# Graph network of 64 graphs: conv2 as nine quarter-rate products over eight graphs at a time

## What is computed

```python
h  = relu(bn2(conv1d(relu(bn1(conv1x1(hT))), conv2_w, pad=8)) + hT)     # x_conv, 17 taps over nodes
s  = h @ w_se.T + b_se;  A = exp(-|s_n - s_m|^2) * adj                   # 3 features
nmp = A @ relu(h @ w_msg.T + b_msg)
r, z, n = GRU gates of [x_conv, nmp] (w_ih) and h (w_hh)
x1 = x + (1 - z) * n + z * h
out = x1 + adj @ (relu(layernorm(x1)) @ weight) + bias
```

## Time and profile before

| | us |
|---|---|
| median of 3 runs | 410.81 (408.74 to 412.92) |
| the profiled execution, its span | 412.3 |
| TensorE busy, by the page | 372.0 (90%) |
| VectorE busy | 327.8 (80%) |
| GpSimd busy | 182.9 (44%) |
| ScalarE busy | 134.7 (33%) |

### The profile page before, as it was taken

One profiled execution on the slowest core, in us unless ns is written; L12 is line 12 of the kernel. 1 busy time (PEld: TensorE's weight loads), 2 busy tenths in 40 slices (PEclk: granted clock), 3 DMA queues, 4 the chain that ended last, 5 costly groups with the idle time before them and its releaser, 6 DMA issues.

```text
span 412.3 us, 7317 instructions
## 1 busy us (share of the span) xinstructions
PE 372.0 (90%) x2460; PEld 335.4 (81%) x2460; DVE 327.8 (80%) x920; ACT 134.7 (33%) x232; POOL 182.9 (44%) x191
## 2 busy tenths in 40 slices
PE   8489497999999999999999999999999999999974
PEld 7377296897979798897979798888979797997953
DVE  5975579679897979879797979879787979778564
ACT  3222132424324242424333342424333242424031
POOL 3973218045271807254361817164461817072402
PEclk9999689999999999999999999999999999999995
DMA  8700000020202020010202020010200000000000
GB/s 305 240 0 0 0 2 0 2 79 2 78 1 76 0 76 0 17 59 0 76 0 76 0 76 0 29 47 0 76 0 25 0 25 0 25 2 14 13 25 26
DMA packets 7933, 15.19 MB, mean 37 GB/s; under 512 B 1008, under 2 KB 1392, under 8 KB 7920
## 3 DMA queue, kind: packets, MB, share of 16 engines
q1 hardware_dynamic: 7632, 14.42, 10.2%
q10 hardware_dynamic: 288, 0.61, 0.4%
HBM read 10.83 MB, written 4.19 MB: 36 GB/s over the span
## 4 chain that ended last, share of the span: by engine, by line
PE 58%; DVE 31%; issue 5%; ACT 3%; DVEq 1%; DMA 1%; POOL 0%; POOLq 0%; ACTq 0%
PE pAC L296 5%; PE pAC L297 5%; PE pAC L298 5%; PE pF L392 4%; PE pH L436 3%; PE pR L296 3%; PE pH L447 3%; DVE h_hi L699 3%; DVE st L625 3%; DVE h_lo L701 3%; DVE st L648 3%; PE pR L298 3%; PE pR L297 3%; PE pZ L297 3%; PE pZ L296 3%
## 5 line engine op out<-in xcount | busy, mean ns | idle before, releaser
L296 PE MATMUL pAC<-c_hi,conv_hi 128*128 128x264 f32 (+1 forms) x288 | 86.8, 301 | 2.5 <-DVE c_lo L713 2.5
L297 PE MATMUL pAC<-c_lo,conv_hi 128*128 128x264 f32 (+1 forms) x288 | 84.0, 292 | 0.0
L298 PE MATMUL pAC<-c_hi,conv_lo 128*128 128x264 f32 (+1 forms) x288 | 83.7, 291 | 0.0
L860 POOL TENSOR_TENSOR base_e<-hTb,A 128x256 f32<-128x256 f32 x16 | 12.7, 794 | 155.7 <-ACT A L531 155.7
L296 PEld LDWEIGHTS pAC<-c_hi,conv_hi 128*128 128x128 f32 x288 | 56.0, 194 | 2.9 <-issue 2.9
L298 PEld LDWEIGHTS pAC<-c_hi,conv_lo 128*128 128x128 f32 x288 | 55.9, 194 | 0.0
L297 PEld LDWEIGHTS pAC<-c_lo,conv_hi 128*128 128x128 f32 x288 | 55.9, 194 | 0.0
L296 PE MATMUL pB<-c_hi,conv_hi 128*128 128x256 f32 x128 | 37.9, 296 | 1.4 <-DVE conv_lo L617 1.4
L297 PE MATMUL pB<-c_lo,conv_hi 128*128 128x256 f32 x128 | 36.7, 287 | 0.0
L298 PE MATMUL pB<-c_hi,conv_lo 128*128 128x256 f32 x128 | 36.6, 286 | 0.0
L572 ACT ACTIVATE msg<-msg_t 128x512 f32<-128x512 f32 x16 | 10.1, 632 | 76.6 <-DVE msg_t L748 76.6
(11 more groups left out here) (187 smaller groups left out, 1015.8 us busy)
## 6 DMA issues: line engine op xcount, KB each, us to landing
x_all<-x_in SPq DMA_DIRECT2D x16, 256.0 KB, 2.8
adj_all<-adj_in SPq DMA_DIRECT2D x16, 256.0 KB, 3.0
...
```

The costliest lines, as they stand in the source:

```text
L296: pe.matmul(acc, w_hi, m_hi, start=start, stop=False)
L297: pe.matmul(acc, w_hi, m_lo, start=False, stop=False)
L298: return pe.matmul(acc, w_lo, m_hi, start=False, stop=stop)
L860: pool.tensor_tensor(base_e[:], phase[:, :, :, 0], A2[:, :, 0:HALF], ALU.add)
```

## The change

conv2 is split twice into even and odd: four phases of nodes, so nine quarter-rate products (X22, X12, X21, X23, X32, X11, X13, X31, X33) with 4 or 5 taps each, 40 taps, each over 8 graphs x 32 columns, three passes: 120 matmuls for eight graphs. They come as pairs in the two banks pP and pQ. Their inputs are differences of phases: px (8 arrays of 128 x 8 x 36) made by `pre` in five instructions on GpSimd (for the first eight graphs on VectorE), rounded by ScalarE in five instructions (`split_hi`) and the low parts made by VectorE in five (`split_lo`). The weights of the products are sums of taps, 37 arrays of 128 columns in place of 25, made on GpSimd, rounded on ScalarE, split on VectorE. The outputs are joined by `s22`, `s12`, `s32` on ScalarE, one instruction on VectorE and four on GpSimd (`base`), then `conv_out` on VectorE, `conv_round` on ScalarE, `conv_lo_out` on VectorE, each in two halves.

The loop has steps of eight graphs (groups a, b in front, p, q in the middle, pp, qq at the back), `for t in range(-1, NS + 1)` with NS = 8: t = -1 has a front alone, t = 0 no back, t = 7 no front, t = 8 a back alone. Nodes are laid phase-major by the host in x, adj and out, so every operand of a product lies in runs of 32. x lies in a ring of eight groups and adj in a ring of six, each slot with its own semaphore. The high part of h is written by ScalarE from PSUM and the low part by VectorE from PSUM. The message bias comes by two matmuls of 264 columns for each group, so the two additions on VectorE go. `left` and `right` have 128 partitions, with zeros below. The second norm's scaling is four instructions on ScalarE in place of four on VectorE and one on ScalarE. The gate weights are split on VectorE. The special order of t = 0 and the halves of the last steps go. `masked`, `pairs`, `right_rows`, `residual`, `finish`, `blend_start`, `blend_end`, `normalise1`, `apply1`, `normalise2` are the old operations on one group each; `with_bias` adds the last bias, `scale1` and `scale2` are the powers.

The products of conv2, before and after:

```diff
-            def conv2_taps(par, product, lo, hi):
-
-                taps = TO if product == 1 else TE
-                acc = (pAC[:, 0:GG * HA], pB[:, 0:W // 2], pAC[:, 0:W // 2])[product]
-                start, width = ((0, HA), (1, HALF), (1, HALF))[product]
-                for k in range(lo, hi):
-
-                    w = k if product == 0 or k == TO and product == 2 else (TE + k if product == 1 else TAPS + k)
-                    last = split_product(acc, conv_hi[:, w * D:(w + 1) * D], conv_lo[:, w * D:(w + 1) * D],
-                                         c1_hi[par][:, product, :, start + k:start + k + width],
-                                         c1_lo[par][:, product, :, start + k:start + k + width],
-                                         start=k == 0, stop=k == taps - 1)
...
+            def product(acc, side, x, weights):
+                for j, w in enumerate(weights):
+                    last = split_product(acc[:, side * CG * QN:(side + 1) * CG * QN],
+                                         conv_hi[:, w * D:(w + 1) * D], conv_lo[:, w * D:(w + 1) * D],
+                                         cx_hi[:, x, :, j:j + QN], cx_lo[:, x, :, j:j + QN],
+                                         start=j == 0, stop=j == len(weights) - 1)
                 return last
...
+            def four(first, more=False):
+                return list(range(first, first + 4)) + ([T16] if more else [])
```

TensorE, the step of eight graphs (the lines taken out are those of the step shown above):

```diff
+            def step(t):
+                a, b, p, q, pp, qq = 2 * t + 2, 2 * t + 3, 2 * t, 2 * t + 1, 2 * t - 2, 2 * t - 1
+                front, middle, back = t + 1 < NS, 0 <= t < NS, t >= 1
+                if t == -1:
                     pe.wait_ge(ident_set, 1)
                     keep_clock(17)
+                if front:
                     x_turn(a)
+                if t == -1:
                     keep_clock(9)
...
+                if back:
+                    o_turn(pp)
+                if middle:
+                    if t == 0:
+                        pe.wait_ge(w_split, 2)
+                    have(pe, cxlo_set, 5 * t + 1)
+                    have(pe, ct_set, 2 * t)
+                    product(pP, 0, X22, four(M22, True))
+                if front:
+                    conv1(a)
+                    messages(a)
+                    x_turn(b)
+                if middle:
+                    have(pe, cxlo_set, 5 * t + 2)
+                    product(pP, 1, X12, four(M12, True)).then_inc(f_done[0], 1)
+                if back:
+                    o_turn(qq)
+                if front:
+                    conv1(b)
+                    messages(b)
                     rows_turn(a)
...
+                if middle:
+                    if t == 0:
+                        pe.wait_ge(w_split, 3)
+                    have(pe, ct_set, 2 * t - 1)
+                    product(pQ, 0, X21, four(M21, True))
+                if front:
                     distances(a)
+                if back:
+                    adj_h2(pp)
+                if middle:
+                    have(pe, cxlo_set, 5 * t + 3)
+                    product(pQ, 1, X23, four(M23)).then_inc(f_done[1], 1)
+                if front:
+                    rows_turn(b)
+                if back:
+                    layer2(pp)
+                if middle:
+                    have(pe, s1_set, t + 1)
+                    product(pP, 0, X32, four(M32)).then_inc(f_done[2], 1)
+                if back:
+                    adj_h2(qq)
+                if front:
+                    distances(b)
                     neighbour_sums(a)
...
+                if middle:
+                    if t == 0:
+                        pe.wait_ge(w_split, 5)
+                    have(pe, cxlo_set, 5 * t + 5)
+                    have(pe, t_set, t + 1)
+                    product(pQ, 0, X11, four(A0) + [T16])
+                if back:
+                    layer2(qq)
+                if middle:
+                    product(pQ, 1, X13, four(A2)).then_inc(f_done[3], 1)
+                if front:
+                    neighbour_sums(b)
+                if middle:
+                    have(pe, s32_set, t + 1)
+                    product(pP, 0, X31, four(A1))
+                    product(pP, 1, X33, four(A3)).then_inc(f_done[4], 1)
+                    for g in (p, q):
+                        gates_h(g)
+                        gates_n(g)
+                        gates_c(g)
```

ScalarE, the part of its step behind the messages of group b:

```diff
+                if back:
+                    second(qq)
+                if front:
+                    decay(a)
+                if t == -1:
+                    round_w(3)
+                    round_w(4)
+                if back:
+                    turned_up(pp)
+                if front:
+                    left_rows(b)
+                if front and t >= 0:
+                    split_hi(t + 1, 0)
+                    split_hi(t + 1, 1)
+                if middle:
+                    have(act, f_done[2], t + 1)
+                    have(act, sumO_set, t)
+                    act.activation(s32[:], pP[:, 0:CG * QN], ACT.Identity, bias=bn_half[:, 0:1],
+                                   scale=bn_a[:, 1:2]).then_inc(s32_set, 1)
+                if back:
+                    turned_up(qq)
+                if front:
+                    decay(b)
+                    sums_hi(a)
+                if front and t >= 0:
+                    split_hi(t + 1, 2)
+                if t == -1:
+                    split_hi(0, 3)
+                    split_hi(0, 4)
+                    act.wait_ge(gate_loaded, 16)
+                    act.activation(gate_hi[:], gate, ACT.Copy).then_inc(gate_rounded, 1)
+                if front:
+                    sums_hi(b)
+                if middle:
+                    conv_round(t, 0)
+                    hidden_gate(p)
+                    conv_round(t, 1)
+                if front and t >= 0:
+                    split_hi(t + 1, 3)
+                    split_hi(t + 1, 4)
+                if middle:
+                    reset_gate(p)
+                    candidate(p)
+                    update_gate(p)
+                    hidden_gate(q)
+                    reset_gate(q)
+                    update_gate(q)
```

The differences of phases (k = 1 to 5), and VectorE:

```diff
+        def pre(eng, t, k):
+            if k == 1:
+                have(eng, c1_set, 2 * t + 2)
+            elif k > 3:
+                have(eng, pre_set, 5 * t + 3)
+            have(eng, cxlo_set, 5 * t)
+            if k == 1:
+                last = eng.tensor_tensor(px[:, X12:X21 + 1], c1[:, 1:3], c1[:, 3:4].to_broadcast([128, 2, CG, QP]),
+                                         ALU.subtract)
+            elif k == 2:
+                last = eng.tensor_tensor(px[:, X32:X23 + 1, :, 0:QP - 1], c1[:, 0:3:2, :, 1:QP],
+                                         c1[:, 3:4, :, 0:QP - 1].to_broadcast([128, 2, CG, QP - 1]), ALU.subtract)
+            elif k == 3:
+                last = eng.tensor_tensor(ac[:], c1[:, 0:2], c1[:, 2:3].to_broadcast([128, 2, CG, QP]), ALU.subtract)
+            elif k == 4:
+                last = eng.tensor_tensor(px[:, X11:X31 + 1], ac[:], px[:, X12:X32 + 1:2], ALU.subtract)
+            else:
+                last = eng.tensor_tensor(px[:, X13:X33 + 1, :, 0:QP - 1], ac[:, :, :, 1:QP],
+                                         px[:, X12:X32 + 1:2, :, 0:QP - 1], ALU.subtract)
+            last.then_inc(pre_set, 1)
...
+            def split_lo(t, k):
+                have(dve, cxhi_set, 5 * t + k + 1)
+                part = slice(*CX_PARTS[k])
+                dve.tensor_tensor(cx_lo[:, part], cx_source(k), cx_hi[:, part].bitcast(F32), ALU.subtract)\
+                   .then_inc(cxlo_set, 1)
...
+            def step(t):
+                a, b, p, q, pp, qq = 2 * t + 2, 2 * t + 3, 2 * t, 2 * t + 1, 2 * t - 2, 2 * t - 1
+                front, middle, back = t + 1 < NS, 0 <= t < NS, t >= 1
+                if back:
+                    blend_start(qq)
+                    residual(pp)
+                if front:
+                    hidden_lo(a)
+                if t == -1:
+                    dve.wait_ge(bias_rounded, 1)
+                    dve.tensor_tensor(bias_r[32:64, :], bias_raw[32:64], bias_r[32:64, :].bitcast(F32), ALU.subtract)\
+                       .then_inc(bias_split, 1)
+                if back:
+                    blend_end(qq)
+                    normalise2(pp)
+                if front:
+                    pairs(a)
+                    hidden_lo(b)
+                if t == -1:
+                    split_w(0)
+                if back:
+                    shift2(pp)
+                    residual(qq)
+                    normalise2(qq)
+                if t == -1:
+                    pre(dve, 0, 1)
+                    split_lo(0, 0)
+                    split_lo(0, 1)
+                    split_w(1)
+                if front:
+                    right_rows(a)
+                    pairs(b)
+                if back:
+                    shift2(qq)
+                if t == -1:
+                    pre(dve, 0, 2)
```

(90 more changed lines are left out.)

1205 lines of the change are left out of this document (559 added, 646 removed).

## The result

| | before | after |
|---|---|---|
| median of the timed runs | 411.87 us (408.74 to 415.74) | 465.51 us (465.28 to 468.79) |
| span of the profiled execution | 412.3 us | 463.6 us |

The changed kernel takes 1.1347 times as long [1.127, 1.1424]; medians here are of all timed runs, but the ratios leave out runs in a second, slower state of the chip, into which two of the four runs of experiment 6 and six of the nine of the kernel before beside experiments 9 to 12 (410.9 to 433.1 us) fell. The forecast had the sign (slower, 437 us) and the mechanism, and not enough of it: 465.5 lies 3.5 us above the range, and the increase is 54 us where 25 were forecast.

The account below looks back on a forecast made before the run. TensorE's own work was taken to bound the kernel before; after, a loop over VectorE and TensorE lengthened by GpSimd port collisions. 51 + 40 + 6 x 49.0 + 36 + 17 = 438 in the span, 437 by the median, range 390 to 462.

Parts of the forecast that it names:

- TensorE 39.3 bare per eight graphs: TensorE's own work in a step of eight graphs, without waits: 39.3 us, down from 46.0.
- VectorE's own work 32.1: VectorE's operations for eight graphs, counted one by one without collisions or waits: 32.1 us.
- Lock-free step 42.6: Loop over VectorE and TensorE without port collisions: 27.9 VectorE work, 5.3 waits, 9.4 from gates_c(p) on, 42.6 us per step.
- Collisions 6.4 (9.3 with GpSimd always first): Some nine meetings of VectorE with GpSimd per step, mean 0.7 each: 6.4 us, 9.3 following the orders with GpSimd first.
- Step 0, 40: First step, without a back: TensorE's 34.8 plus low clock and waits, 40 us.
- End, 17: Last stage: one chain of full-width operations without halves, the other group's between them, 17 us to the last byte.
- rival C: The wait at gates_c(p), some 7 us, also lowers TensorE's clock: step 53, sum 462 us; chance 0.12 (above 455).
- Step 7, 36: Step without a front: 32 of matmuls, 2 waiting for second(qq), 1 to 2 at the gates, 36 us.
- Start, 51: VectorE's queue ahead of x_turn(2) holds everything of the first front, so conv2 begins near 51 us instead of 19.1.
- The signs to look for: In the profile after, TensorE's longest waits: gates_c for xc_lo, then rows_turn(b) behind exp(a), and gates_h(q) for tz.
- A: Rival: port collisions cost almost nothing, VectorE mostly getting the port first; 144 + 6 x 42.6 = 400 us; chance 0.22.
- B: Rival: TensorE stays the bound, all waits hidden; 144 + 6 x 39.3 = 380 us; chance 0.08.

Follow-up runs that it names:

- experiment 6: The kernel before with only left and right widened to 128 partitions, zeros below, so distances is a 128-row matmul: 436.96 us, ratio 1.04.
- experiments 9 to 12: Kernel before with 128-row left/right and h's parts from PSUM, 401.06 us; then experiment 8 with one edit undone each: 433.31, 393.24, 392.52 us.
- experiment 8: Changed kernel with apply1 behind the conv output, second(qq) and candidate(p) later on ScalarE, GpSimd held until pairs(b), start reordered: 389.23 us.
- experiment 1: Changed kernel with GpSimd's phase differences, base additions and last bias cut to an eighth of their columns or less from step 0: 410.52 us.
- experiment 2: Changed kernel with both apply1 on VectorE moved behind the conv output: 444.97 us, ratio 1.0736.

## Why the prediction was right or wrong

- **TensorE 39.3 bare per eight graphs**: near. 40.20 of 40.80 in experiment 8. Of the 0.9, the two `distances` (0.34 and 0.32 where I had said about 0.25) are 0.2, and 120 conv2 products at 0.126 to 0.133 instead of 0.1225 are 0.4 to 1.3.
- **VectorE's own work 32.1**: 30.95 in experiment 1. **Lock-free step 42.6**: 42.9, and its parts held too: 33.2 up to `gates_c(p)` against 33.3, 9.4 behind it against 9.6. Counting the queue held to 1%, with a little luck: blend(p) stands in the loop at 2.8 where the list of VectorE's part has 2.0 and 1.35; with 3.35 the step comes to 42.05.
- **VectorE busy near 39 of 49**: 38.74 of 51.5.
- **Collisions 6.4 (9.3 with GpSimd always first)**: 7.2 ahead of `xc_lo`, the low clock behind `rows_turn(b)` included. The total was fair, and in part luck, since the picture behind it (nine meetings at a mean of 0.7) was not: two places make up 5.2, `pairs(b)` with 3.1 and `apply1` with 2.1.
- **What failed** is not the mechanism but terms of the sum, which came to 438 where the span is 463.6. The plainest is step 0, where the prediction did not apply its own mechanism; the end, the half clock, step 7 and the start follow.
- **Step 0, 40**: took 47.9, the largest miss of one stage. I had summed TensorE's 34.8, clock and waits, and put nothing for collisions there, though GpSimd works beside VectorE in step 0 too. TensorE waited 5.75 at `gates_c(p)` and went on at half clock. In experiment 1, without GpSimd's columns, step 0 takes 40.6, and in experiment 8 38.6.
- **End, 17**: 23.0. Its length was estimated and never counted: 20.6 in experiment 1 and 20.5 in experiment 8, so 3.6 of the 6.0 were missing from the chain itself and 2.4 came with GpSimd's columns. The chain has second() with four ScalarE instructions (1.65 instead of some 1.1), holes of 2.99, 3.72 and 2.87, and half clock for `adj_h2` and `layer2` (0.60 in the mean over the last 23 us).
- **The half clock, nothing in the sum**: I had kept it as a price of rival C alone (a wait of some 7 us at `gates_c(p)`). In the step of t = 3 the clock read 0.50 after 3.54 us of idling, and after 3.03 too. Behind `gates_c(p)` it costs 1.7, 1.4 and 0.7 in three of the settled steps and nothing in the two where the clock stayed up, 0.75 in the mean. The 50.9 of a settled step are thus 0.3 more of lock-free loop, 0.8 more of collisions and 0.75 of clock than the 49.0. What the low clock behind `rows_turn(b)` costs in the kernel after was not separated from the collisions.
- **Step 7, 36**: 38.8, and 36.4 in experiment 1: again GpSimd's columns, which I had counted for the settled steps alone.
- **Start, 51**: 54.6. The order of VectorE's queue was as described. `apply1(1)` took 6.25 over the three weight sums (done at 18.4, put at 17), and `conv1(0)` ran at half clock.
- **The signs to look for** came as named: `gates_c(p)` for `xc_lo`, then `rows_turn(b)` behind exp(a), and `gates_h(q)` for tz where the first is gone (experiment 2). Left out of the sum was what these waits do to the clock.
- **The rivals**: A (400) and B (380) didn't hold for the change as it stands. Without GpSimd's columns the span is 408.0 (experiment 1), so even with no collisions A's sum was 8 too low. B's number was nonetheless near for what the same instructions can do in another order: 386.4 span in experiment 8. C is not the case either: its hole of 7 didn't come (3.5 in the settled steps, 5.75 in step 0), its clock did in part.

On the port, the prediction said that no row shows a scalar_tensor_tensor with two SBUF inputs blocked. Here is one, at the end; both inputs, mv and rs, lie in SBUF (timeline, VectorE and GpSimd):

```profile
449.98 1.26 POOL L989 TENSOR_TENSOR work<-work,late 128x512 f32<-128x512 f32 x1
450.05 1.22 DVE L801 SCALAR_TENSOR_TENSOR nb<-mv,rs 128x4 f32<-128x4 f32 x1 [1.12 <-POOL rs L965]
```

Four elements take 1.22 us, where the same line takes 0.15 beside no GpSimd instruction. The Trainium skill (SBUF — State Buffer, Who interferes with whom) says that only the shared port pair causes contention and that it is an exclusive lock; the row agrees, and extends what the earlier trace rows shows to this form.

What stays open: why a VectorE instruction that starts 0.01 us after a GpSimd one passes and one that starts 0.09 after it waits; why the same hole on TensorE is followed by half clock in one step and not in the next; and how the 5.3 us of waits on ScalarE and powers that I counted divide, since experiment 1 shows only that the whole of the loop is right.
